# Attention as one straight block with its loading woven in, four score banks and two side banks

## What is computed

```python
B, T, D, NUM_HEADS, HEAD_DIM = 4, 1024, 128, 16, 64
xn = layernorm(x)                              # (4, 1024, 128)
q, k, v = (xn @ w.T for w in (wq, wk, wv))     # split into 16 heads of 64
q, k = rope(q), rope(k)
scores = where(causal, q @ k.T * HEAD_DIM**-0.5, -inf)
out = softmax(scores) @ v                      # per batch and head
x = x + layernorm(concat_heads(out) @ wo.T)
x = x + layernorm(ffn(layernorm(x)))
```

## Time and profile before

| | |
|---|---|
| median of 3 runs | 1382.13 us (1374.25 to 1384.11) |
| the profiled execution | 1379.8 us, span 1378.1 us |
| TensorE busy | 1162.7 us, 84% |
| VectorE, ScalarE, GpSimd busy | 1019.6, 928.1, 963.3 us |
| mean granted clock of TensorE | 0.944 |
| attention until its last block end | 1081.9 us |

### The profile page before, as it was taken

How to read it: one execution, slowest core, us unless ns; L and a number is a source line. 1 busy time by engine, 2 the same in 40 slices (tenths; PEclk the granted TensorE clock), 3 DMA queues, 4 the chain that set the end, 5 groups by cost and what they waited for, 6 DMA issues and landing times. The chain is left out here.

```text
span 1378.1 us, 34881 instructions
## 1 busy us (share of the span) xinstructions
PE 1162.7 (84%) x13560; PEld 799.0 (58%) x13560; DVE 1019.6 (74%) x2176; ACT 928.1 (67%) x2036; POOL 963.3 (70%) x998
## 2 busy tenths in 40 slices
PE   2447989999798989979998988999899388898984
PEld 0214766767476766756676766667677245565652
DVE  7856878778486878767787877778674467787857
ACT  1114877787677887777877877787889564454543
POOL 3435988888687988868888987888767433454523
PEclk9678999999899999999999999999999799999997
DMA  5275143443514152523415261541400400000002
GB/s 183 53 176 123 37 119 78 124 102 70 124 33 124 35 136 63 139 69 88 111 46 139 54 137 44 124 113 44 124 3 2 120 11 0 2 1 1 0 0 61
DMA packets 53364, 103.84 MB, mean 75 GB/s; under 512 B 6608, under 2 KB 23248, under 8 KB 51152
## 3 DMA queue, kind: packets, MB, share of 16 engines
q1 hardware_dynamic: 53200, 101.61, 29.8%
HBM read 63.18 MB, written 37.22 MB: 73 GB/s over the span
## 5 line engine op out<-in xcount | busy, mean ns | idle before, releaser
L573 POOL TENSOR_TENSOR Plo<-P,Phi 128x512 f16<-128x512 f32 (+3 forms) x640 | 537.5, 866 | 169.0 <-ACT P L364 168.4
L361 ACT ACTIVATE Phi<-psS 128x512 f16<-128x512 f32 (+3 forms) x768 | 387.9, 505 | 166.7 <-PE psS L249 122.4
L364 ACT ACTIVATE P<-psS 128x512 f32<-128x512 f32 (+3 forms) x640 | 309.5, 484 | 0.0
L263 PE MATMUL psO<-V,Phi 128*128 128x65 f16 x2304 | 290.1, 194 | 0.5 <-issue 0.5
L267 PE MATMUL psO<-V,Plo 128*128 128x65 f16 x2304 | 290.3, 195 | 0.0
L265 PE MATMUL psO<-V,Phi 128*128 128x64 f16 x2304 | 289.6, 193 | 0.0
L243 PE MATMUL psS<-Q,K 128*128 128x512 f16 (+3 forms) x768 | 254.6, 332 | 35.7 <-DVE Plo L423 17.3
L457 DVE TENSOR_REDUCE pmax<-psX 128x1 f32<-128x512 f32 x384 | 252.8, 683 | 21.6 <-PE psX L303 11.5
L303 PE MATMUL psX<-K,Q 128*128 128x512 f16 (+3 forms) x768 | 231.6, 329 | 28.9 <-DMA Q<-q_way 17.5
L246 PE MATMUL psS<-Q,K 65*128 65x512 f16 (+3 forms) x768 | 255.4, 333 | 0.0
L263 PEld LDWEIGHTS psO<-V,Phi 128*128 128x128 f16 x2304 | 220.8, 99 | 40.4 <-POOL Plo L573 3.3
(11 more groups left out here) (172 smaller groups left out, 2228.5 us busy)
## 6 DMA issues: line engine op xcount, KB each, us to landing
K<-k_way SPq DMA_DIRECT2D x48, 512.0 KB, 7.1
k_way<-HL SPq DMA_DIRECT2D x64, 256.0 KB, 3.9
q_way<-HL SPq DMA_DIRECT2D x64, 256.0 KB, 4.0
Q<-q_way SPq DMA_DIRECT2D x64, 256.0 KB, 7.3
Q<-q_way SPq DMA_DIRECT2D x16, 512.0 KB, 12.1
x<-in_x SPq DMA_DIRECT2D x4, 512.0 KB, 7.4
out<-x SPq DMA_DIRECT2D x8, 256.0 KB, 2.3
y<-in_x SPq DMA_DIRECT2D x3, 512.0 KB, 5.5
```

What stands on the lines that cost most here:

```text
L263: nc.tensor.matmul(O, M.Phi[:, U % NP_, k * P:(k + 1) * P], V[:, HD:2 * HD + 1], start=j == 0 and k == 0, stop=False, skip_group_check=True)
L361: nc.scalar.activation(M.Phi[:, U % NP_, 0:w], X, ACT.Exp, scale=SCALE)
L364: nc.scalar.activation(full, X, ACT.Exp, scale=SCALE).then_inc(S.exp_done, 1)
L573: nc.gpsimd.tensor_tensor(M.Plo[:, U % NP_, 0:w], M.P32[:, U % NP_, 0:w], M.Phi[:, U % NP_, 0:w], ALU.subtract).then_inc(S.lo_pool, 1)
```

## The change

All blocks of the attention but the block end behind it become one. Slots are numbered from -2 to 15 without a loop, and `plan` lays them out in one table. `NS` goes from 3 to 4, `NAUX` from 3 to 2. The maxima stand at steps 8 to 39 in place of 8 to 43, the join at 40 in place of 43, `mt` at 43 in place of 44. Slot -2 has 12 steps with its rotations one step apart. Slot -1 has its own steps, the maxima one each from step 7.

x of all batches is loaded into `y`, which loses its spare batch. The first batch is normalised by VectorE at the start; the other 24 tiles get their statistics in slot -1 at step 6 and are normalised there by ScalarE (steps 26 to 33). A new side item `ln` transposes half a batch into a side bank and splits it into `xT`; for batches 1 to 3 it stands at steps 23 and 30 of slots 1, 5 and 9. `x_way`, `xq` and `xv` are gone. The weights' float32 copies lie in `P32`. The memset of the row of constants in `K2` (VectorE) is now a DMA from `scale_row`; the memsets of `On`, `OT` and `y` are gone. The first keys and queries go from `HL` straight into `K1`, `K2`, `Q1`, `Q2` by 48 DMAs of 32 partitions. In slot -2 VectorE makes the second sum of the rotation in place of GpSimd.

```diff
-NS = 3
+NS = 4
...
-LN_STEPS = (3, 12, 21, 30, 31)
+LN_STEPS = (23, 30)
-MX_FIRST, MX_LAST, JOIN_STEP, MT_STEP = 8, 43, 43, 44
+MX_FIRST, MX_LAST, JOIN_STEP, MT_STEP = 8, 39, 40, 43
+QK_EARLY = ((2, 3, 4, 5, 6, 7, 8, 9), (0, 1, 2, 3, 10, 12, 17, 19))
+V_EARLY, MX_EARLY = (4, 5, 23, 27), 7
+EARLY_STEPS = 12
+X_STATS, X_RECIPROCAL, X_NORMAL = 6, 9, 26
...
-NAUX = 3
+NAUX = 2
...
+    steps = [(-2, u) for u in range(EARLY_STEPS)]
+    steps += [(s, u) for s in range(-1, LAST + 1) for u in range(SU)]
+    steps += [(LAST + 1, u) for u in range(LAG + OUT_LAG + 1)]
...
+                if kind == "ln":
+                    batch, half = a
+                    if batch == 0:
+                        pe.wait_ge(S.norm_first, half + 1)
+                    else:
+                        pe.wait_ge(S.norm_later, TT * (batch - 1) + HT * (half + 1))
+                    for k in range(HT):
+                        mm = nc.tensor.transpose(X[:, k * P:(k + 1) * P], M.y[:, batch * TT + HT * half + k, :],
+                                                 M.ident[:])
...
+                if n == 0 and s == -1:
+                    if which == 0:
+                        act.wait_ge(S.first_k, 16 * 4 * GH)
+                        act.wait_ge(S.first_k2, 16 * 2 * GH)
...
+                if s == -1 and u == X_STATS:
+                    for b in range(1, B):
+                        dve.wait_ge(S.x_load[b + 1], 16)
+                    variance(range(TT, NT))
+                    dve.wait_ge(S.consts, 3)
...
+                        if s == -2:
+                            taken(dve, item)
+                            if r > 0:
+                                dve.wait_ge(S.rope_lo, r)
+                            nc.vector.tensor_tensor(M.R[:, 1, :], M.R4[:, 2, :], M.R4[:, 3, :],
+                                                    ALU.add).then_inc(S.rope_part, 1)
...
+            def first_keys():
+
+
+                sp.wait_ge(S.rope_lo, 2)
+                for h in range(GH):
+                    rows = slice(h * HALF, (h + 1) * HALF)
+                    for k in range(4):
+                        sp.dma_start(M.K1[k * HALF:(k + 1) * HALF, 0, h, :],
+                                     M.HL[rows, 0, k, :]).then_inc(S.first_k, 16)
+                for h in range(GH):
+                    rows = slice(h * HALF, (h + 1) * HALF)
+                    for k in range(2):
+                        sp.dma_start(M.K2[k * HALF:(k + 1) * HALF, 0, h, :],
+                                     M.HL[rows, 0, k, :]).then_inc(S.first_k2, 16)
...
-        attention_block(nc, M, S, 0, [-2, -1], [-1], [-2, -1])
-        block_end(nc, S)
-        slots = list(range(GROUPS))
-        with nc.Fori(0, B - 1) as b:
-            attention_block(nc, M, S, b, slots, slots, slots)
-            block_end(nc, S)
-        attention_block(nc, M, S, B - 1, slots, slots[:-1], slots[:-2], flush=True)
+        attention_block(nc, I, M, S)
         block_end(nc, S)
```

More of the change, by code:

```diff
@@ L101, in put @@
         at.setdefault((slot, step), []).append((slot,) + item)
-    for s in slots:
-        if s >= 0:
+    for half in range(2):
+        put(-2, half, ("ln", 0, half))
+    for s in range(-2, LAST + 1):
+        if s >= 1:
             for half in range(2):
@@ L222, in halves_at, with rope_items @@
         return []
+    def rope_items(s, u, early, later):
+        return [x for x in at.get((s, u - (early if s < 0 else later)), []) if x[1] == "qk" and x[4] == 1]
     with nc.Block() as blk:
@@ L313, in side @@
                     own = s - 1 if c == 1 else s
[L314 removed]
+                    if half == 0:
                         pe.wait_ge(S.out_scaled, HALVES * (GH * own + 2 * (c + 1)))
@@ L418, in _, with then, variance @@
         @blk.vector
         def _(dve):
+            done = [0]
+            def then(ins):
+                done[0] += 1
+                ins.then_inc(S.stats, 1)
+                dve.wait_ge(S.stats, done[0])
+            def variance(tiles):
+                for t in tiles:
+                    last = nc.vector.bn_stats(M.bn[:, t, :], M.y[:, t, :])
+                then(last)
+                for t in tiles:
+                    last = nc.vector.bn_aggr(M.mv[:, t, :], M.bn[:, t, :])
+                then(last)
+                span = slice(tiles[0], tiles[-1] + 1)
+                nc.vector.tensor_scalar(M.std[:, span], M.mv[:, span, 1], EPS, None, ALU.add).then_inc(S.var_ready[0], 1)
@@ new lines, in first_normal @@
+            def first_normal(half):
+                tiles = slice(half * HT, (half + 1) * HT)
+                dve.wait_ge(S.std_ready[0], half + 1)
+                then(nc.vector.reciprocal(M.rstd[:, tiles], M.std[:, tiles]))
+                for t in range(half * HT, (half + 1) * HT):
+                    last = nc.vector.tensor_scalar(M.y[:, t, :], M.y[:, t, :], M.mv[:, t, 0:1], M.rstd[:, t:t + 1],
+                                                   ALU.subtract, ALU.mult)
+                last.then_inc(S.norm_first, 1)
@@ L564, in _ @@
                     out_scale(Uw, n)
-                for item in at.get((s, u), []) if s == GROUPS else []:
+                for item in at.get((s, u), []) if s > LAST else []:
                     side(item)
@@ L817, in phase_attention, with block_end @@
+def block_end(nc, S):
+    nc.sync.sem_clear(range(S.first, S.last + 1))
+    nc.all_engine_barrier()
 def phase_attention(nc, I, M, S, sb, ps):
```

613 lines of the change are left out of this document (272 added, 341 removed).

## The result

The changed kernel takes 1398.57 us (median of 4 runs, 1396.63 to 1400.1), the kernel before 1381.95 beside it. The ratio is 1.013 [1.0087, 1.0172]: slower by 1.3%, where 1351 was forecast and 1390 was the end of the range. The profiled execution took 1396.63, its span 1394.9 us with a mean clock of 0.953, so it is compared with the 1378.1 of the earlier trace rows.

What follows compares the result with a forecast made beforehand. TensorE was taken as the bound, VectorE not far behind. From 1379.8: start -31.8, block ends -25.4, loading later batches +6, steady slots +21.7, last two slots -1.5 gave 1348.8, with 2.3 for the median 1351 us; range 1316 to 1390.

Steps and rivals of the forecast that it cites:

- Link (2): Start: the first rotation's four blocks take 4.45 us each, so keys are ready at 23.3 and queries at 32.2.
- Link (3): Start: SyncE issues 24 small transfers each for keys and queries at 0.5 us; keys landed by 37.5.
- Link (6): Start: the maxima before the first exp, from first product to join, take 33 us, ending at 85.4.
- (c): Steady slot: the fourth score bank removes TensorE's wait for a score bank, -1.0 us a slot.
- (e): Steady slot: four steps lose their maximum, so ScalarE sets the pace there, +0.6 us a slot.
- (b): Steady slot: the clock no longer falls at the wait for joined maxima in seven slots, -0.85 us on average.
- (d): Steady slot: with two side banks TensorE waits for readers of side items, +5.1 us a slot, bounds 3 and 9.
- (a): Steady slot: transposing later behind the last reduction removes TensorE's wait for joined maxima (`rmax`), -2.3 us a slot.
- Rival 2: Steady slots: two side banks tie TensorE to VectorE, 9 us a slot or more, 1407 us and upward; chance 0.12.
- Rival 1: Steady slots: two side banks cost little, 2 us a slot in place of 5.1, giving 1308 us; chance 0.17.
- Rival 4: Start gets no shorter: small transfers at 1.3 us land keys 19 us later, giving 1383 us; chance 0.14.
- Rival 3: Slots: many short TensorE waits bring half clock in two stretches a slot, 47 us more, 1398 us; chance 0.06.

Runs made afterwards that it cites:

- e8: The changed kernel with the statistics of the 24 tiles at step 4 of slot -1 in place of 6; 1391.8 us, ratio 1.0079.
- e1: The changed kernel with three score banks and three side banks in place of four and two; 1315.8 us, ratio 0.9545.
- e5: The changed kernel with three score banks in place of four, two side banks kept, one bank idle; 1414.9 us, ratio 1.0246.
- e2: The kernel before with four score banks and two side banks, nothing else changed; 1455.5 us, ratio 1.0556.
- e4: The kernel before with maxima at steps 8 to 39, join at 40, transpose at 43, three and three banks; 1362.3 us, ratio 0.9888.
- e3: The changed kernel with maxima back at steps 8 to 43, join at 43, transpose at 44; 1389.1 us, ratio 1.0074.
- e7: The changed kernel, four and two banks, with the long side items moved to steps further apart; 1376.2 us, ratio 0.9966.
- e6: The changed kernel with two score banks and four side banks; 1382.9 us, ratio 1.0026.
- e10: The changed kernel with three and three banks, statistics at step 4, maxima to step 41, join 41, transpose 44; 1328.3 us, ratio 0.9625.

## Why the prediction was wrong, point by point

**The start, -31.8 on record, -21.8 measured.** The chain was right, its terms were too short.
- Link (2), 4.45 us a block: in after GpSimd starts its first subtractions at 15.38, 20.70, 25.89 and 31.21, 5.3 apart. 1.77 - 1.26 = 0.5 of this is the exclusion shown above, which the text counted as hidden, over four blocks the 2 us that its side sentence gave; the rest is 0.27 of waiting for VectorE and the handovers. Keys were ready at 25.7, not 23.3.
- Link (3), 0.5 us a small transfer: the 24 issues of the keys took 10.09 + 5.03 = 15.1 us, 0.63 each, inside the bounds of 0.25 and 0.72, with +3 us. SyncE's rows:

```profile
25.77 10.09 SPq L715 DMA_DIRECT2D K<-HL  x16
35.91 5.03 SPq L720 DMA_DIRECT2D K<-HL  x8
```

- Link (5), the statistics ahead of the first maximum, 6.9 on record and 6.6 measured, is right, as e8 shows by moving them. The first maximum came at 57.1 (52.4).
- Link (6), 33 us for the maxima, took 38.1, to the join at 95.2. TensorE has 1.2 GHz for nearly all of it: clock 0.54.

```profile
57.00:95.20 38.20, 29.26 (x96) 9.91 (x96) 30.37 (x50) 12.62 (x29) 9.21 (x6) 0.54 0.24 56
```

The banks alone change this. In e1 the maxima take 57.4 to 89.2, 31.8 us, at a clock of 0.86:

```profile
57.40:89.20 31.80, 20.99 (x92) 7.96 (x92) 28.63 (x52) 12.62 (x29) 9.22 (x6) 0.86 0.29 67
```

In e5, with three score banks like e1 but two side banks, they take 37.5 us at 0.59. So the two side banks cost these maxima some 6 us. The lower clock need not be most of it: in e2 the same stretch takes 35.9 us at 0.79, in before 30.9 at 0.83. Link (7) was 4.7 on record and is 99.95 - 95.18 = 4.8.

**Block ends and loading: right.** The 25.4 us are gone, and the `ln` items cost 1.6 to 2.0 us in each of slots 1, 5 and 9 (65.4 to 65.8 against 63.8), where 2 was on record. This is where the one straight block earns what it was built for.

**A steady slot, +1.55 on record, +4.3 measured.** This is the step that failed: the fourteen slots took 34 of the 48 us by which the span is longer than forecast (the start has 10, the last two slots 4.6). Of its terms (c) is 1.0 by e5 and held, (e) was not seen apart, and of (b) this much holds, that the clock is at 1.00 in the steady slots of after, with no fall as in the earlier trace rows. Two terms were mis-sized, by about the same:
- (d), 5.1 for the two side banks (its pieces add up to 5.0), is 6.3 by the slots of e5 and e1. The walk itself was sound where it looked. TensorE's score products in e5 fall behind those of e1 by 1.2 us in steps 8 to 13 (1.2 on record), by 2.5 in steps 18 to 22 (2.4) and by 1.5 in steps 26 to 30 (1.4), in slot 6 and in every other from 1 to 13. But they fall behind by 0.6 at steps 15 and 16 and by 0.8 at steps 23 and 24 as well (0.4 there in slots 1, 5 and 9), where the walk found nothing. 36 maxima in 32 steps mean that four steps have two (8, 15, 23, 31), and the walk was made on the *old* spacing, where no step has two. That the doubled steps cause these two shifts is likely by their place, but no run moved them alone. In four of the thirteen slots the tail then makes up 0.6 to 1.0. The bounds of 3 and 9 did hold the term.
- (a), (b) and (e), together -2.55 for the new range of the maxima, are -1.3 by e4, with three side banks. The wait for `rmax` is gone there, and so are the falls of the clock at the joins, but the waits for a score bank grew by 15.0 us, 1.1 a slot. That term was not in the sum at all: the text priced the density only at the head's pace, (e), +0.6. With two side banks the difference of e3 and after is even +0.3.

Together the two make some 2.5 of the 2.75 us that a slot lacks.

**The last two slots** were to gain 1.5 and lost 3.1. The fourth score bank did what it was to do (slot 15, 40.4 for 42.1; without it, in e5, 42.1), but slot 14 prepares slot 15's maxima and takes 55.9 us where it took 51.1: two side banks cost there too, and the forecast counted them in 14 slots only.

**The signs of being wrong** that were on record did not warn. A slot of 63.8 us lies under 64, the first exp at 99.95 before 100, and the clock held in the slots, though the time is 48 us off: each bound left so much room that the errors could add up inside them.

**The rivals.** Rival 2, two side banks that tie TensorE to VectorE, named the mechanism. Its own threshold (8.3 us a slot) was not met, with 6.3; what brought the time past it was the missing gain of (a) and (b) and the 10 us at the start. Its price of 1407 and more was not reached. Its reason for, VectorE's 38.9 of 42.6 us, was not the cause: VectorE is idle 10 us in the middle of the slot, and e7 gets 22 us back with the same load. Rival 1, the opposite, falls with e1. Rival 4 falls too: the issues cost 0.63, not 1.3. Rival 3, the clock, gave 1398, and the measured time is the same by chance: its mechanism is refuted in the slots, where TensorE is idle 7.3 us, in pieces of up to 1.1 us, and the granted clock stays 1.00. The rule of the Trainium skill that was named with it (page TensorE: Matmul & The Clock Gate, section A second HAM failure mode: psum-queue depth-cycling) therefore does not show in the steady slots of this kernel.

In slot -1, which rival 3 did not speak of, the clock did go with the banks: from the first maximum to the join it is 0.54 to 0.70 in the kernels made from after with two side banks, and 0.82 to 0.89 in those with three or four. What stays open is how the lower clock there comes about, and what part of the 6 us is its own.

## What to carry to other kernels

A bank of a rotating pool is worth what the item's reader needs beyond the writer's next item. Count it for both pools by the items that are held longest: here a rotation half is read twice and V waits for a copy on ScalarE. The waits of before named the two pools alike, 17 us for a score bank and 13 for a side bank, but a fourth score bank was worth 16 us and the third side bank 99: waits with a bank present do not price its lack. Nor is a score bank cheap as such, since with two of them e6 lost what the straight block had won. If a change gives one pool's bank to the other, make the walk over all items in the *new* order, doubled steps included, since the stalls come from the pairs that stand close. And where a wait is removed by compressing work, look for the wait that grows beside it: in e4 more than a third of the gain went there.

## What the runs showed of the hardware that was not expected

- Small transfers from SBUF to SBUF of 32 partitions cost the queue's engine 0.63 us each to issue, where one of 256 KB to DRAM costs 0.72 in the earlier trace rows: a quarter of the bytes saves an eighth of the issue time.
- VectorE and GpSimd with two float32 SBUF operands each do not overlap: 1.26 becomes 1.77 or 2.17, and 1.21 becomes 2.28, by who comes first.
- Some dozen waits of TensorE a slot, of up to 1.1 us (1.5 in one slot), left the granted clock at 1.00 through the steady slots of after. One wait a slot of up to 2.7 us, like the one of the earlier trace rows, went with the fall of the earlier trace rows in seven slots of before, and in nine slots of e10 (up to 3.0 us); but e3 has such a wait in every slot too, 30.1 us in all, and the clock falls in two. So such a wait goes with the fall without being enough for it.
